# Splitting GpSimd's addition for the softmax sum into three pieces, in the attention of an audio tower on one Trainium2 core

## The chip, the cores and the metric

One Trainium2 chip, one NeuronCore of it. TensorE (PE) multiplies matrices into PSUM, VectorE (DVE), ScalarE (ACT) and GpSimd (POOL) work elementwise, SyncE (SP) starts transfers. The engines run their own instruction streams and meet at semaphores. The metric is the device time of one execution of the whole program, in microseconds (us); lower is better.

## The reference

The program is a small audio tower over 16 clips of 746 frames with 128 features: a convolution over 5 frames with batch norm, a delta-rule attention, an expert-choice FFN, a cross attention against 64 videos of 12 frames each, and a routed FFN. The change is in the cross attention, which comes down to this:

```python
t = layer_norm(text_embeds, ln1_g, ln1_b)        # the tower's rows, T = 16 clips, Nw = 746 rows each
vd = layer_norm(video_embeds, ln1_g, ln1_b)      # V = 64 videos, Fr = 12 frames
q = (t @ Wq.T + bq).reshape(T, Nw, HEADS, HEAD_DIM)      # 2 heads of 64
k = (vd @ Wk.T + bk).reshape(V, Fr, HEADS, HEAD_DIM)
v = (vd @ Wv.T + bv).reshape(V, Fr, HEADS, HEAD_DIM)
logits = jnp.einsum('avhd,bthd->abhvt', k, q) / math.sqrt(HEAD_DIM)
weights = jax.nn.softmax(logits, axis=3)         # over the 12 frames of a video
attn = jnp.einsum('avhd,abhvt->abhtd', v, weights)
attn = attn.mean(axis=0)                         # over the videos
o = attn @ Wo.T + bo
```

So for each of the tower's rows, head and video there is a softmax over 12 frames. Its sum is what the change is about.

## The kernel before, in words

The rows of the 16 clips are cut into 96 chunks (NCH), six a clip: five of 128 rows and one of 106. The attention phase goes over the chunks n = 0 to 95 in one software pipeline that each engine has unrolled for itself. The 128 partitions hold 2 heads x 64 videos; the free dimension holds the 12 frames (FR) times the chunk's rows.

The stations of chunk n, with their lines:

- TensorE writes the logits for 12 frames into three PSUM banks (L1710, 24 matmuls, interleaved with the 24 of the weighted values of chunk n-4, L1718). Two sets of three banks alternate.
- VectorE takes the negated maximum over the frames (L1607) into `nm`.
- TensorE adds `nm` to the logits in PSUM, three matmuls for four frames each (L1737, semaphore `shifted`).
- ScalarE takes the exponential in three instructions for four frames each (L1658) into `eb[:, n % 4]` in SBUF; each raises `e_ready` by one.
- GpSimd adds frames 0 to 5 and frames 6 to 11 in one addition (L1681) into `t1[:, n % 2]`, six partial sums a row. It waits for all three exponentials of the chunk, and, as `t1` has two buffers, for VectorE to have read the partial sums of chunk n-2 (`summed`). It raises `tree`.
- VectorE adds up the six partial sums (L1603) into `den`, once `tree` allows.
- ScalarE turns `den` into its reciprocal by a logarithm and an exponential (L1667, L1669).
- VectorE multiplies the 12 frames of exponentials by it in place (L1612), semaphore `w_ready`.
- TensorE multiplies by the values (L1718), ScalarE copies the result (L1648), TensorE multiplies by Wo and adds the bias (L1748, L1749), ScalarE copies that out (L1644).

VectorE's order is fixed: in its step n it does the sum of chunk n-2, the maximum of chunk n, the multiply of chunk n-2. TensorE's step n is the block of logits n and values n-4 (it first waits for the multiply of chunk n-4), then in some steps a transposition (L367) or a query projection (L1688) for the next clips, then the shift of chunk n-1, then the output of chunk n-5. ScalarE's step n does the copies, the exponentials of chunk n-1, the logarithm and its inverse for chunk n-2, and in some steps three normalizations (L1623) for the next clips. GpSimd has nothing but the addition.

Of the kernel before, what the change touches and what calls it, by code (L numbers as in the profile page):

```python
# [7 lines left out]
ALU = mybir.AluOpType  # L8
# [1516 lines left out]
def attention_phase(nc, k):  # L1525
# [6 lines left out]
    with stack:  # L1532
# [4 lines left out]
        t1 = sb("t1", [P, 2, P, 6])  # L1537
# [7 lines left out]
        q_ps, q_ready, q_bias, l_ps, m_ready, shifted, e_ready = (  # L1545
            sem(x) for x in ("q_ps", "q_ready", "q_bias", "l_ps", "nm_ready", "shifted", "e_ready"))
        tree, summed, rd_ready, w_ready, a_ps, a_ready, o_ps, o_ready = (
            sem(x) for x in ("tree", "summed", "rd_ready", "aw_ready", "a_ps", "a_ready", "ao_ps", "ao_ready"))
        logged = sem("logged")
        ST = 2 * NC  # L1550
        FB = FR // 3
# [5 lines left out]
        def lbanks(n):  # L1557
            o = 3 * (n % 2) * 512
            return k.psf[:, o:o + FR * P].rearrange("p (v t) -> p v t", t=P)
# [4 lines left out]
        def wide(n):  # L1564
            return rows(n % NC)
# [13 lines left out]
        with nc.Block() as block:  # L1579
            @block.vector  # L1580
            def _(dve):
                nc.vector.tensor_scalar(bq8[:], k.bq[:, 0:1], 0.125, None, ALU.mult).then_inc(q_bias, 1)
                nc.vector.memset(ones[:], 1.0).then_inc(q_bias, 1)
                nc.vector.tensor_copy(bparts[:, 0, :], k.bo1[:, :]).then_inc(q_bias, 1)
                for s in range(2):
                    rest = k.bo1[:, :] if s == 0 else rd[:, 0, :]
                    dve.wait_ge(q_bias, 2 * s + 3)
                    nc.vector.tensor_tensor(rd[:, s, :], rest, bparts[:, s, :], ALU.subtract).then_inc(q_bias, 1)
                    dve.wait_ge(q_bias, 2 * s + 4)
                    nc.vector.tensor_copy(bparts[:, s + 1, :], rd[:, s, :]).then_inc(q_bias, 1)  # L1590
                nc.vector.tensor_scalar(bo3[:, :], bparts[:, 0, :], k.ident[:, 0:1], None, ALU.mult).then_inc(q_bias, 1)
                for s in (1, 2):
                    dve.wait_ge(q_bias, 7 + s)
                    nc.vector.scalar_tensor_tensor(out=bo3[:, :], in0=bparts[:, s, :], scalar=k.ident[:, s:s + 1],
                                                   in1=bo3[:, :], op0=ALU.mult, op1=ALU.add).then_inc(q_bias, 1)
                for n in range(NCH + 2):
                    w = n - 2
                    if 0 <= w < NCH:
                        dve.wait_ge(tree, w + 1)
                        m = wide(w)  # L1600
                        if w >= 2:
                            dve.wait_ge(logged, w - 1)
                        nc.vector.tensor_reduce(den[:, w % 2, 0:m], t1[:, w % 2, 0:m, :], AX_X,  # L1603
                                                ALU.add).then_inc(summed, 1)
                    if n < NCH:
                        dve.wait_ge(l_ps, n + 1)
                        nc.vector.tensor_reduce(nm[:, n % 2, 0:wide(n)],  # L1607
                                                lbanks(n)[:, :, 0:wide(n)].rearrange("p v t -> p t v"), AX_X,
                                                ALU.max, negate=True).then_inc(m_ready, 1)
                    if 0 <= w < NCH:  # L1610
                        dve.wait_ge(rd_ready, w + 1)
                        nc.vector.tensor_tensor(eb[:, w % 4, :, 0:m], eb[:, w % 4, :, 0:m],  # L1612
                                                rd[:, w % 2, None, 0:m].to_broadcast([P, FR, m]),
                                                ALU.mult).then_inc(w_ready, 1)
                dve.wait_ge(o_ready, NCH)
# [58 lines left out]
            @block.gpsimd  # L1674
            def _(pool):
                for n in range(NCH):
                    e, m = eb[:, n % 4], wide(n)
                    pool.wait_ge(e_ready, 3 * n + 3)
                    if n >= 2:
                        pool.wait_ge(summed, n - 1)  # L1680
                    nc.gpsimd.tensor_tensor(t1[:, n % 2, 0:m, :].rearrange("p t v -> p v t"), e[:, 0:6, 0:m],  # L1681
                                            e[:, 6:12, 0:m], ALU.add).then_inc(tree, 1)

            @block.tensor
            def _(pe):
# [721 lines left out]
```

## Time and profile before

| | us |
|---|---|
| median of 3 runs | 2271.65 |
| lowest and highest | 2266.53, 2272.15 |
| the profiled execution | 2271.49 |
| its span in the profile | 2269.7 |
| attention phase in it | about 1070 to 1524 |

The profile records one execution of the program. Engines are named PE, PEld (TensorE's loading of weights), DVE, ACT and POOL; L12 is line 12 of the kernel. A group of instructions is told with its count, the time that it keeps its engine busy, the mean duration of one in ns, and the idle time of the engine just before it with what ended that idle time. In a timeline a row is a run of equal instructions: when it starts (in us from the span's start), how long it lasts, and in brackets how long the engine sat idle before it and which instruction released it. Ends of matmuls are modelled, so a row of PE may end slightly after the next has started.

### The profile page before, as it was taken

Reading aid. Unit: us, or ns where it says so; the run is one execution under the profiler, and the core shown is the slowest. Engines: PE = TensorE matmul, PEld = TensorE weight load, DVE = VectorE, ACT = ScalarE, POOL = GpSimd, SP = SyncE. Lnnn points to the kernel's source line nnn. Section 1 sums busy time; section 2 is a strip of 40 time slices with the busy share of each in tenths; the row PEclk is TensorE's granted clock in tenths of the full one; section 3 lists DMA queues with packets and bytes.
Section 4 is the critical chain, followed back from the end, with each engine's and each line's share of the span. In section 5 each row is a group of like instructions: output and inputs, shape, how many; then the busy total and the mean of one; then the engine's idle time right before and its main releaser. Section 6 shows DMA issues by size and latency. Waiting matters only on the chain. (4 is left out here: it accounts for less than half of the span.)

```text
span 2269.7 us, 54561 instructions
## 1 busy us (share of the span) xinstructions
PE 2015.7 (89%) x20890; PEld 1786.3 (79%) x20890; DVE 1604.5 (71%) x4095; ACT 1071.8 (47%) x2699; POOL 602.3 (27%) x649
## 2 busy tenths in 40 slices
PE   6699999989746888996999999986999999999998
PEld 5488777779545787884777777766999999999998
DVE  4755555663583765665999999986777777777774
ACT  4433333332344565652676777753444444444443
POOL 0002222220005545520333334333212212221220
PEclk9699999999976999997999999997999999999999
DMA  8100000000221111100000000000000000000000
GB/s 186 43 1 12 11 12 11 11 11 1 67 59 40 41 34 40 40 22 1 3 3 3 3 3 3 3 3 1 8 14 7 7 7 14 7 7 14 7 8 15
DMA packets 80354, 44.50 MB, mean 20 GB/s; under 512 B 45800, under 2 KB 74024, under 8 KB 79752
## 3 DMA queue, kind: packets, MB, share of 16 engines
q1 hardware_dynamic: 74248, 29.53, 5.7%
q0 software_dynamic: 5888, 12.07, 2.0%
q8 instruction: 136, 2.23, 0.4%
q14 instruction: 82, 0.67, 0.1%
HBM read 27.20 MB, written 14.38 MB: 18 GB/s over the span
## 5 line engine op out<-in xcount | busy, mean ns | idle before, releaser
L2127 ACT ACTIVATE w<-banks,b 128x384 f32<-128x384 f32 (+1 forms) x512 | 259.3, 571 | 392.9 <-PE banks L2202 392.9
L2184 PE MATMUL banks<-w,w 128*128 128x128 f32 (+1 forms) x3072 | 364.1, 275 | 0.0
L2184 PEld LDWEIGHTS banks<-w,w 128*128 128x128 f32 (+1 forms) x3072 | 350.4, 189 | 9.1 <-issue 8.7
L1710 PE MATMUL banks<-qT,w 64*64 64x128 f32 (+1 forms) x4608 | 268.0, 269 | 13.2 <-DVE eb L1612 8.7
L1710 PEld LDWEIGHTS banks<-qT,w 64*64 64x64 f32 x4608 | 247.4, 134 | 31.0 <-issue 20.8
L1718 PE MATMUL banks<-eb,w 64*64 64x128 f32 (+1 forms) x4608 | 268.9, 270 | 1.0 <-DVE eb L1612 1.0
L1681 POOL TENSOR_TENSOR t<-eb 128x768 f32<-128x768 f32 x96 | 172.0, 1791 | 289.2 <-ACT eb L1658 286.6
L1718 PEld LDWEIGHTS banks<-eb,w 64*64 64x64 f32 x4608 | 244.1, 133 | 1.7 <-DVE eb L1612 1.5
L2024 DVE SCALAR_TENSOR_TENSOR h<-banks,t_wt,h 128x128 f32 (+3 forms) x672 | 183.5, 341 | 83.3 <-PE banks L2184 79.8
L1237 POOL DMA_INDIRECT xg<-xs,rowu x184 | 178.8, 972 | 127.5 <-DMA xg<-xs,rowu 83.6
L1612 DVE TENSOR_TENSOR eb<-eb,rd 128x1536 f32<-128x1536 f32 x96 | 210.8, 2196 | 2.3 <-ACT rd L1669 2.3
L2200 PE MATMUL banks<-t_xh,t_w1h 128*128 128x384 f32 (+1 forms) x512 | 182.4, 356 | 0.5 <-ACT w L2106 0.5
L2202 PE MATMUL banks<-t_xh,t_w1l 128*128 128x384 f32 (+1 forms) x512 | 171.4, 335 | 0.0
L1607 DVE TENSOR_REDUCE nm<-banks 128x128 bf16<-128x1536 f32 x96 | 162.8, 1696 | 11.4 <-PE banks L1710 11.4
L2201 PE MATMUL banks<-t_xlo,t_w1h 128*128 128x384 f32 (+1 forms) x512 | 170.8, 334 | 0.0
L2067 POOL TENSOR_TENSOR t_rstd<-t_nv,t_minus_half 128x6 f32<-128x6 f32 x48 | 63.6, 1325 | 393.9 <-DVE t_nv L1925 392.5
L1658 ACT ACTIVATE eb<-banks 128x512 f32<-128x512 f32 (+1 forms) x288 | 146.9, 586 | 0.6
L1183 DVE SCALAR_TENSOR_TENSOR x_yl<-banks,gates,x_yh 128x128 fp32r<-128x128 f32 x184 | 52.0, 344 | 132.7 <-ACT x_yh L1330 128.0
L1428 PE MATMUL banks<-x_sel,x_yh 128*128 128x374 f32 (+1 forms) x384 | 119.3, 392 | 2.1 <-ACT x_oT L1339 2.1
L1191 DVE TENSOR_SCALAR x_sel<-iota,place 128x748 fp32r<-128x748 f32 x184 | 106.6, 633 | 4.0 <-PE banks L1428 4.0
L729 ACT ACTIVATE DT<-banks 128x768 f32<-128x768 f32 x60 | 48.6, 810 | 123.4 <-PE banks L822 123.4
L1428 PE MATMUL banks<-x_sel,x_yl 128*128 128x374 f32 (+1 forms) x384 | 98.9, 339 | 0.0
(305 smaller groups left out, 4261.3 us busy)
## 6 DMA issues: line engine op xcount, KB each, us to landing
out<-h SPq DMA_DIRECT2D x16, 320.0 KB
xs<-r_xl SPq DMA_DIRECT2D x16, 192.0 KB, 2.7
h<-in_xT SPq DMA_DIRECT2D x4, 750.0 KB, 14.9
h<-in_xT SPq DMA_DIRECT2D x4, 749.0 KB, 17.9
xg<-xs,rowu POOLq DMA_INDIRECT x184
xs<-r_xl SPq DMA_DIRECT2D x16, 128.0 KB
blocks<-NT SPq DMA_DIRECT2D x24, 48.0 KB, 1.9
D<-blocks SPq DMA_DIRECT2D x24, 48.0 KB, 2.0
```

The costliest lines, as they stand in the source:

```text
L1237: nc.gpsimd.indirect_dma_start(out=xg[:, 4 * g + j, :], out_offset=None, in_=k.xs, in_offset=bass.IndirectOffsetOnAxis(ap=rowu[:, col:col ...
L1428: last = nc.tensor.matmul(k.ps[:, 5 + s, 0:TW // 2], y[lo:hi, col % 8, :], sel[lo:hi, col % SEL, s * (TW // 2):(s + 1) * (TW // 2)], start ...
L1612: nc.vector.tensor_tensor(eb[:, w % 4, :, 0:m], eb[:, w % 4, :, 0:m], rd[:, w % 2, None, 0:m].to_broadcast([P, FR, m]), ALU.mult).then_inc ...
L1681: nc.gpsimd.tensor_tensor(t1[:, n % 2, 0:m, :].rearrange("p t v -> p v t"), e[:, 0:6, 0:m], e[:, 6:12, 0:m], ALU.add).then_inc(tree, 1)
L1710: last = nc.tensor.matmul(lbanks(n)[place(n, hd), v, 0:wide(n)], k.Kt[half(hd), v, :], qT[half(hd), n // NC % 2, (n % NC) * P:(n % NC) * P ...
L1718: last = nc.tensor.matmul(k.ps[half(hd), 6, 0:wide(a)], k.Vd[place(a, hd), v, half(hd)], eb[place(a, hd), a % 4, v, 0:wide(a)], start=(v = ...
L2024: last = nc.vector.scalar_tensor_tensor(out=hh, in0=k.psf[0:n, o:o + P], scalar=wt[0:n, par, c * E1 + e:c * E1 + e + 1], in1=hh if e else ...
L2127: nc.scalar.activation(gb[u % 2][:, f, s * GW:s * GW + NFREE[s]], k.ps[:, order.bank(n), 0:NFREE[s]], ACT.Relu, bias=k.b1_1[:, 2 * e + f:2 ...
L2184: last = nc.tensor.matmul(k.psf[0:n, o:o + P], gb[u % 2][:, f, c * P:c * P + n], k.w2_1[:, 2 * e + f, :], start=(f == 0), stop=(f == 1))
L2200: nc.tensor.matmul(ps, w1h[:, 2 * e + f, :], xh[:, g, 0:w], start=True, stop=False)
L2201: nc.tensor.matmul(ps, w1h[:, 2 * e + f, :], xlo[:, g, 0:w], start=False, stop=False)
L2202: nc.tensor.matmul(ps, w1l[:, 2 * e + f, :], xh[:, g, 0:w], start=False, stop=True).then_inc(full, 1)
```

## The change

GpSimd's addition of chunk n becomes three. Each waits for one of ScalarE's exponentials (four frames), adds the first two of its frames to the last two, and writes two of the six partial sums. The pairing of the frames becomes another one, the sum of all twelve is the same. VectorE now waits for three counts of `tree` a chunk. The wait for `summed` comes ahead of the first piece.

```diff
                     if 0 <= w < NCH:
-                        dve.wait_ge(tree, w + 1)
+                        dve.wait_ge(tree, 3 * w + 3)
                         m = wide(w)
...
                 for n in range(NCH):
                     e, m = eb[:, n % 4], wide(n)
-                    pool.wait_ge(e_ready, 3 * n + 3)
                     if n >= 2:
                         pool.wait_ge(summed, n - 1)
-                    nc.gpsimd.tensor_tensor(t1[:, n % 2, 0:m, :].rearrange("p t v -> p v t"), e[:, 0:6, 0:m],
-                                            e[:, 6:12, 0:m], ALU.add).then_inc(tree, 1)
+                    for s in range(3):
+                        pool.wait_ge(e_ready, 3 * n + s + 1)
+                        v = s * FB
+                        nc.gpsimd.tensor_tensor(t1[:, n % 2, 0:m, 2 * s:2 * s + 2].rearrange("p t v -> p v t"),
+                                                e[:, v:v + 2, 0:m], e[:, v + 2:v + 4, 0:m], ALU.add).then_inc(tree, 1)
```

`FB` is 4, the frames of one exponential.

## Rows read from the trace of the kernel before

**Rows 1.** The page, sections 1 and 5: engines, and the multiply.

```profile
PE 2015.7 (89%) x20890; PEld 1786.3 (79%) x20890; DVE 1604.5 (71%) x4095; ACT 1071.8 (47%) x2699; POOL 602.3 (27%) x649
...
L1612 DVE TENSOR_TENSOR eb<-eb,rd 128x1536 f32<-128x1536 f32 x96 | 210.8, 2196 | 2.3 <-ACT rd L1669 2.3
```

**Rows 2.** Busy time by window: stretch, length, each engine, TensorE's clock, DMA.

```profile
1200.00:1300.00 100.00, 95.31 (x2266) 74.65 (x2257) 100.00 (x66) 69.46 (x188) 39.30 (x22) 1.00 0.01 3
```

**Rows 3.** Waits of TensorE, 1100 to 1490 us: total, times, longest.

```profile
PE banks L1710 <- DVE eb L1612: 7.2, 14, 0.5
```

**Rows 4.** Waits, 1490 to 1524 us, the drain.

```profile
PE banks L1710 <- DVE eb L1612: 1.0, 3, 0.5
PE banks L1718 <- DVE eb L1612: 1.0, 3, 0.4
```

**Rows 5.** Timeline of VectorE, 1280 to 1300 us.

```profile
1284.50 2.20 DVE L1612 TENSOR_TENSOR eb<-eb,rd 128x1536 f32<-128x1536 f32 x1
1286.63 0.94 DVE L1603 TENSOR_REDUCE den<-t 128x128 f32<-128x768 f32 x1
1287.49 1.74 DVE L1607 TENSOR_REDUCE nm<-banks 128x128 bf16<-128x1536 f32 x1
1289.16 2.49 DVE L1612 TENSOR_TENSOR eb<-eb,rd 128x1536 f32<-128x1536 f32 x1
...
1293.83 1.78 DVE L1612 TENSOR_TENSOR eb<-eb,rd 128x1536 f32<-128x1536 f32 x1
...
1298.06 1.74 DVE L1612 TENSOR_TENSOR eb<-eb,rd 128x1536 f32<-128x1536 f32 x1
```

**Rows 6.** Timeline of GpSimd, 1280 to 1300 us.

```profile
1283.26 1.83 POOL L1681 TENSOR_TENSOR t<-eb 128x768 f32<-128x768 f32 x1 [2.82 <-ACT eb L1658]
1288.21 1.84 POOL L1681 TENSOR_TENSOR t<-eb 128x768 f32<-128x768 f32 x1 [3.11 <-ACT eb L1658]
1292.16 1.84 POOL L1681 TENSOR_TENSOR t<-eb 128x768 f32<-128x768 f32 x1 [2.12 <-ACT eb L1658]
```

**Rows 7.** Timeline of TensorE, 1282 to 1311 us, around the starts of blocks.

```profile
1282.36 0.33 PE L1710 MATMUL banks<-qT,w 64*64 64x128 f32 x2
...
1290.80 0.44 PE L1749 MATMUL banks<-wo,aT 128*128 128x128 f32 x2
1291.75 0.33 PE L1710 MATMUL banks<-qT,w 64*64 64x128 f32 x2 [0.51 <-DVE eb L1612]
...
1295.14 0.44 PE L1749 MATMUL banks<-wo,aT 128*128 128x128 f32 x2
1295.66 0.33 PE L1710 MATMUL banks<-qT,w 64*64 64x128 f32 x2
...
1310.01 0.33 PE L1710 MATMUL banks<-qT,w 64*64 64x128 f32 x2
```

**Rows 8.** Exponentials: timeline of ScalarE, then their group, 1085 to 1520 us.

```profile
1286.57 1.56 ACT L1658 ACTIVATE eb<-banks 128x512 f32<-128x512 f32 x3
...
1290.51 1.57 ACT L1658 ACTIVATE eb<-banks 128x512 f32<-128x512 f32 x3
...
L1658 ACT ACTIVATE eb<-banks 128x512 f32<-128x512 f32 x235 | 122.7, 598 | 0.6
```

**Rows 9.** GpSimd's additions by shape: count, busy us, mean ns, idle us before.

```profile
L1681 POOL TENSOR_TENSOR t<-eb 128x768 f32<-128x768 f32 x80 | 147.0, 1837 | 251.7 <-ACT eb L1658 249.1 <-DVE den L1603 2.6
...
L2078 POOL TENSOR_TENSOR t_ol<-t_ol,g 128x384 f32<-128x384 f32 x32 | 33.0, 1030 | 21.4 <-DVE t_ol L1935 21.4
L2080 POOL TENSOR_TENSOR t_ol<-t_ol,b3n 128x384 f32<-128x384 f32 x32 | 32.0, 1001 | 2.5
...
L1681 POOL TENSOR_TENSOR t<-eb 128x636 f32<-128x636 f32 x16 | 25.0, 1560 | 37.5 <-ACT eb L1658 37.5
...
L645 POOL TENSOR_TENSOR Db<-eye,Nb 96x256 f32<-96x256 f32 x6 | 5.2, 858 | 278.7 <-DMA Nb<-blocks 278.7
...
L653 POOL TENSOR_TENSOR Db<-Db,outer 96x56 f32<-96x56 f32 x12 | 3.5, 293 | 0.9
```

## The prediction

> **What bounds the kernel now.** I read the page first. TensorE leads with 2015.7 us of 2269.7, and VectorE's multiply in attention (L1612) has a mean of 2196 ns [rows 1]. The change touches attention alone, so I asked for a window of it: between 1200 and 1300 us TensorE is busy 95.31 and VectorE 100.00 of 100 us at full clock, GpSimd 39.30 [rows 2]. Two engines look like the bound; the waits say which end last. Over fourteen groups of six chunks TensorE waits 7.2 us for VectorE's multiply, 14 times, at most 0.5 [rows 3]; in the drain it waits 1.0 + 1.0 more [rows 4]. So what any change of the softmax sum can give back is about this wait, however full VectorE looks: behind it TensorE's own work is the floor.
>
> Then the rows of one group, chunk by chunk. The reader is to see a pattern that repeats to 0.01 us. A block (logits of chunk n interleaved with values of chunk n-4) starts at 1282.36 for n = 46, and the same place in the next group (n = 52) starts at 1310.01: 27.65 us for six chunks [rows 7]. In it TensorE stops twice. Before the block at 1291.75 (n = 48) its last matmul ended at 1290.80 + 0.44 = 1291.24: 0.51 idle. Before the block at 1295.66 (n = 49) it was free at 1295.14 + 0.44 = 1295.58: 0.08 idle, too short for the table of waits. The group's floor is 27.65 - 0.59 = 27.06 us.
>
> What ended both stops is a multiply: 1289.16 + 2.49 = 1291.65 and 1293.83 + 1.78 = 1295.61 [rows 5]. Why are they this long? The multiply at 1298.06 took 1.74; GpSimd's additions of rows 6 end before it starts. Those at 1284.50, 1289.16 and 1293.83 were issued while an addition ran, and each ends 1.61 after that addition: 1283.26 + 1.83 = 1285.09 and 1286.70; 1288.21 + 1.84 = 1290.05 and 1291.65; 1292.16 + 1.84 = 1294.00 and 1295.61 [rows 5, 6]. The multiply (two operands in SBUF) does nothing until the addition (two operands in SBUF) is over. The max on PSUM stays at 1.74 under the same additions. So TensorE's wait is pinned to the end of an addition, and the addition to ScalarE: it starts 0.08 after the third exponential (1286.57 + 1.56 = 1288.13, then 1288.21) [rows 6, 8].
>
> **The change, part by part.** *Removed:* the wait for all three exponentials. The first ends one mean, 0.60, after its start [rows 8]: at 1287.17 instead of 1288.13, so GpSimd may start 0.96 us earlier. It is idle then, so nothing is in its way.
>
> *Added:* two more instructions, 256 elements a partition each instead of 768. No row has this shape in this use. 768 elements took 1837 ns and 636 took 1560 (128 and 106 time steps), 2.10 ns an element and 226 fixed; 384 took 1030 in L2078 and 1001 in L2080, 56 took 293 in L653, so 2.25 or 2.16 an element [rows 9]. By the first pair a third costs 226 + 256 x 2.10 = 0.76 us, by L2078 and L653 293 + 200 x 2.25 = 0.74, by L2080 and L653 0.72, the lower bound. The upper bound is the 96x256 row itself, 0.86. A gap between two instructions of GpSimd: L2080, which waits for L2078, sat idle 2.5 us over 32, 0.08 each; where the semaphore has long been raised it may be nothing. I take 0.74 and 0.04 a gap, so 3 x 0.74 + 2 x 0.04 = 2.30 for the sum against 1.84. Starting 0.96 earlier and lasting 0.46 longer, it ends 0.5 earlier. Bounds: 3 x 0.72 = 2.16 (ends 0.64 earlier) and 3 x 0.86 + 0.16 = 2.74 (ends 0.06 earlier). The exponentials come 0.5 apart, faster than the pieces, so only the first piece ever waits for ScalarE.
>
> *Moved:* the wait for the earlier sum now stands ahead of piece one. VectorE had read the sums of two chunks before (1286.63 + 0.94 = 1287.57) 3.6 us ahead of the first piece at 1291.19 that reuses their buffer, so it costs nothing; the cover is that distance [rows 5]. No DMA, no order of another queue moves.
>
> *What it is worth, in the group of the rows.* Pieces start at 1287.17 + 0.08 = 1287.25 and end at 1289.55; the multiply ends at 1291.16, and block 48 can start 0.10 later (1291.65 to 1291.75 is that step): 1291.26 against 1291.24. The wait of 0.51 falls to 0.02. Next, the exponentials at 1290.51 are not moved, since they precede block 48. First one ends 1291.11, pieces 1291.19 to 1293.49, multiply 1295.10, block 49 at 1295.15. TensorE's own time from block 48 to the end of its work is 1295.58 - 1291.75 = 3.83, so it would be ready at 1295.09: 0.06 is left. The group saves 0.59 - 0.08 = 0.51. Both waits occur 15 times (blocks 6 to 90): 15 x 0.51 = 7.7 us.
>
> The multiply must also be issued in time. VectorE's steps are 0.86 (sum, 1286.63 to 1287.49), 1.67 (max, to 1289.16) and 1.67 (multiply without a block) [rows 5]: 4.20 a chunk, 25.2 a group, below 27.06. It has almost 2 us of room a group, which the blocking eats; what is late next is TensorE itself.
>
> *Drain.* The last chunks carry no normalization, TensorE needs some 3.9 a chunk and VectorE 4.2, so VectorE binds and an earlier sum only removes the overlap. Of the 2.0 us waited there [rows 4] I take 0.5 (bounds 0 and 1.0).
>
> Sum: 7.7 + 0.5 = 8.2 us off 2271.49 (the profiled execution, span 2269.7), hence **2263.3**; the median 2271.65 is within 0.2 of it.
>
> A rule against the change: by the Trainium skill, "SBUF — State Buffer", section "Who interferes with whom", a VectorE instruction with two SBUF inputs and a GpSimd one that reads SBUF exclude each other, and whoever issues first holds the shared ports for its whole instruction. The trace agrees for an addition that came first (1.61 above); no row has a multiply first. By this rule a multiply could slip ahead of a piece and hold the rest back 1.74, a case priced below from rows.
>
> **Rivals.** *The pieces are dear:* each costs the 96x256 row's 0.86 plus 0.08. The sum ends at 1287.25 + 2.74 = 1289.99, block 48 starts at 1291.70, and a group saves 0.06 or so: 15 x 0.06 = 1 us, 2270.5. For: GpSimd's small instructions have the largest fixed share. Against: 56 elements took only 293 ns, so that fixed share is at most 0.2 [rows 9]. This is also the case in which the change gains nothing of what it is made for.
>
> *Full recovery:* pieces at 0.72 without gaps, or multiplies that go between pieces and need not wait for the third. All 0.59 and the drain's 1.0: 15 x 0.59 + 1.0 = 9.9 us, 2261.6.
>
> *Slower, the multiply goes first:* today each addition holds the ports through; three leave gaps. No row has a multiply first, so I take the blocking as mutual: a piece issued under a multiply waits for its end. Suppose the multiply of block 48 is issued just before piece one, at 1287.2, ends at 1288.95, and the pieces, at the dear price, run from there to 1291.7. The next sum starts 1291.8, max (short chunk, 1.4) ends at 1294.05, but the following chunk's pieces started only at 1291.7 and end 1294.45; that multiply ends 1296.06, block 49 at 1296.1 against 1295.66 today: 0.45 lost a group, 15 x 0.45 = 6.8 us, 2278.3. At 0.74 a piece the same order gives 1288.95 + 2.30 = 1291.25, sum and max until 1293.6, pieces until 1293.55, multiply until 1295.35: still 0.3 gained. So it decides only from about 0.85 a piece, and only if VectorE runs over 1 us ahead. A late sum would also hold ScalarE's logarithm and the copies behind it, which feed TensorE.
>
> **How the numbers follow.** Forecast (2262 to 2265) 0.52; full recovery 0.12; dear pieces or half the gain 0.28; multiply first 0.08. A measurement of this kernel can't tell less than 0.3%, 6.8 us. Faster than that: the full case and most of the forecast, 0.57, since the group's gain needs only 0.42 of 0.59. Same: dear pieces, half gains and the forecast's lower edge, 0.35. Slower 0.08. The range 2260 to 2271 leaves out the multiply-first case and the far end of each side.
>
> **What would show it.** 288 additions at L1681's place, 0.7 to 0.8 us each, GpSimd's time there from 147.0 + 25.0 = 172 to some 215 us [rows 9]. TensorE's wait for the multiply in the steady stretch from 7.2 to under 2 us, and the group from 27.65 to about 27.14. Multiplies still ending 1.61 after the last piece that blocked them. It is wrong if a piece takes over 0.85; if a multiply starts inside the gaps and the following piece shows 2.4 us instead of 0.74; if the sums over t1 start waiting for GpSimd often; or if TensorE finds another wait in the place of the one removed, on ScalarE's copies first.

## The result and the profile after

The changed kernel takes 2258.51 us (median of 6 runs, 2256.72 to 2259.81) against 2270.85 for the kernel before (6 runs, 2266.53 to 2272.15): a ratio of 0.995, 95% interval 0.994 to 0.996, so 9 to 14 us faster. The forecast was 2263.3, with a range from 2260 to 2271. The direction and the mechanism held; the time lies 1.5 us below the range.

First, how much of it lies where the change is. The attention phase, from the first block of logits to the start of the last block of values, in the timelines of TensorE. Before:

```profile
1069.88 3.46 PE L1710 MATMUL banks<-qT,w 64*64 64x128 f32 x30 [0.76 <-ACT qT L1629]
...
1521.32 0.91 PE L1718 MATMUL banks<-eb,w 64*64 64x106 f32 x15
```

And after, where the same instructions are two lines further down:

```profile
1066.99 6.24 PE L1712 MATMUL banks<-qT,w 64*64 64x128 f32 x72 [0.76 <-ACT qT L1629]
...
1508.07 0.67 PE L1720 MATMUL banks<-eb,w 64*64 64x106 f32 x10
```

1521.32 - 1069.88 = 451.4 us before, 441.1 after: 10.4 us less. What lies behind is the same to 0.1 us (2269.7 - 1521.3 = 748.4 and 2256.4 - 1508.1 = 748.3). Ahead of attention this profile is 2.9 us shorter; the repeat (e0) shows whether that is of the change.

Busy time by window after, for the stretch of [rows 2]:

```profile
1200.00:1300.00 100.00, 97.63 (x2339) 77.08 (x2330) 98.20 (x68) 71.52 (x194) 46.59 (x68) 1.00 0.01 3
```

TensorE rose from 95.31 to 97.63 of 100 us. VectorE, which had no idle time before, now has 1.80 us of it: between 1100 and 1480 us its multiply waits 5.1 us in all for ScalarE's reciprocal, of which more at the end. TensorE's waits after, 1097 to 1477 us, which answers to [rows 3]; this is the whole list:

```profile
PE banks L1750 <- ACT a_xT L381: 5.8, 28, 0.2
```

The 7.2 us behind the multiply are gone. The 5.8 us for ScalarE's copy (L381) stood in the list before too, as L1748, with the same 28 times: some 0.4 us of a group's floor is this wait and not TensorE's own work. GpSimd and VectorE after, then TensorE at the same two blocks, 48 and 49, as in [rows 5 to 7]:

```profile
1279.93 2.13 POOL L1683 TENSOR_TENSOR t<-eb 128x256 f32<-128x256 f32 x3 [2.81 <-ACT eb L1658]
1283.88 2.12 POOL L1683 TENSOR_TENSOR t<-eb 128x256 f32<-128x256 f32 x3 [1.82 <-ACT eb L1658]
```

```profile
1281.33 2.33 DVE L1612 TENSOR_TENSOR eb<-eb,rd 128x1536 f32<-128x1536 f32 x1
...
1285.83 1.77 DVE L1612 TENSOR_TENSOR eb<-eb,rd 128x1536 f32<-128x1536 f32 x1
```

```profile
1283.43 0.44 PE L1751 MATMUL banks<-wo,aT 128*128 128x128 f32 x2
1283.88 0.33 PE L1712 MATMUL banks<-qT,w 64*64 64x128 f32 x2
...
1287.27 0.44 PE L1751 MATMUL banks<-wo,aT 128*128 128x128 f32 x2
1287.72 0.33 PE L1712 MATMUL banks<-qT,w 64*64 64x128 f32 x2
```

A row "x3" is now the three pieces of a chunk. They end at 1279.93 + 2.13 = 1282.06, and the multiply 1.60 later, at 1283.66; the next at 1286.00 and 1287.60. So the multiply is still held until the last piece is over, as before. But 1283.66 is now ahead of 1283.87, when TensorE is done with its own work, and 1287.60 ahead of 1287.71. Both blocks start at once. The group from block 46 to block 52 runs from 1274.98 to 1302.01, here with the block's first row at each end:

```profile
1274.98 0.33 PE L1712 MATMUL banks<-qT,w 64*64 64x128 f32 x2
...
1302.01 0.33 PE L1712 MATMUL banks<-qT,w 64*64 64x128 f32 x2
```

27.03 us against 27.65: the group lost 0.62. The two waits came 15 times, so fifteen such groups are 9.3 us; the drain (from block 91 to the last one) went from 32.06 to 31.13 us, the first steps (to the start of block 5) from 23.82 to 23.72.

### The profile page after: what moved, and what is told of

The parts are those of the page before. It is cut to its first block and busy times, and to the rows that moved or that the text cites. A ratio compares the mean times of both kernels' runs of the same rounds, so it can differ in the third digit from the quotient of the medians.

```text
span 2256.4 us, 54753 instructions
## 1 busy us (share of the span) xinstructions
PE 2009.5 (89%) x20890; PEld 1782.2 (79%) x20890; DVE 1585.7 (70%) x4095; ACT 1071.1 (47%) x2699; POOL 631.8 (28%) x841
## 5 line engine op out<-in xcount | busy, mean ns | idle before, releaser
L1683 POOL TENSOR_TENSOR t<-eb 128x256 f32<-128x256 f32 (+1 forms) x288 | 199.7, 726 | 250.9 <-ACT eb L1658 213.0
L1612 DVE TENSOR_TENSOR eb<-eb,rd 128x1536 f32<-128x1536 f32 x96 | 192.0, 2000 | 9.3 <-ACT rd L1669 8.1
```

Source lines behind the costliest of these rows:

```text
L1683: nc.gpsimd.tensor_tensor(t1[:, n % 2, 0:m, 2 * s:2 * s + 2].rearrange("p t v -> p v t"), e[:, v:v + 2, 0:m], e[:, v + 2:v + 4, 0:m], ALU. ...
```

## The experiments

Eight kernels. "Attention" is the stretch defined above, "group" the six chunks from block 46, both from each one's own trace.

| kernel | median us | ratio to before, 95% | attention us | group us | attention starts at |
|---|---|---|---|---|---|
| before | 2270.85 | | 451.4 | 27.65 | 1069.9 |
| changed | 2258.51 | 0.995 (0.994 to 0.996) | 441.1 | 27.03 | 1067.0 |
| e0, changed again | 2260.64 | 0.9949 (0.9933 to 0.9966) | 441.0 | 27.03 | 1071.2 |
| e1, three late | 2274.68 | 1.0023 (1.0011 to 1.0036) | 455.3 | 28.04 | 1072.3 |
| e2, two pieces | 2263.80 | 0.9977 (0.9965 to 0.9989) | 446.6 | 27.38 | 1067.4 |
| e3, four pieces | 2275.39 | 1.0026 (1.0015 to 1.0036) | 457.7 | 28.04 | 1068.2 |
| e4, one small | 2259.90 | 0.9945 (0.9928 to 0.9963) | 438.1 | 27.01 | 1071.9 |
| e5, fill | 2255.15 (one run) | | 440.1 | 27.01 | 1064.5 |
| e6, multiply first | 2382.53 | 1.0498 (1.0477 to 1.052) | 569.4 | 35.10 | 1062.1 |
| e7, query in the block | 2270.95 | 0.9998 (0.9987 to 1.0009) | 452.4 | 27.79 | 1072.5 |

The ratios are to runs of the kernel before on the same chip, in two batches: median 2268.87 (29 runs) for e0 to e3 and 2270.37 (17 runs) for e4 to e7; they are not exact quotients of the medians.

### e0: the changed kernel again

> The changed kernel once more, unaltered. In its first profile attention (from the first block of logits to the last block of values) took 441.1 us against 451.4 before, and what lies ahead of attention was 2.9 us shorter as well. Theory: only the 10.4 us in attention belong to the change, and the stages ahead of it vary by some us between executions whatever the kernel. Expected: attention 441.1 within 0.3, the part ahead of it anywhere between 1066 and 1071 us. Rival: the shorter part ahead is of the change too; then it starts attention at 1067.0 within 0.5 again.

Attention took 441.0 us again, and this time started at 1071.2. So the 10.4 us are the change's. The further 2.9 us of the first profile are not: the same kernel started attention at 1067.0 and at 1071.2, and the kernel before at 1069.9, between the two. Over all kernels the last column runs from 1062.1 to 1072.5, though none of them changes anything ahead of attention.

### e1: three pieces, but late

```diff
-                        pool.wait_ge(e_ready, 3 * n + s + 1)
+                        pool.wait_ge(e_ready, 3 * n + 3)
```

> Three pieces, but all of them behind the third exponential. Theory (the end of the last addition alone sets TensorE's wait, through the blocked multiply): the three take 2.12 us where the one took 1.84, so the sum ends 0.28 later than before the change; a group of six chunks takes 27.65 + 0.27 = 27.9 us, attention 456, the whole some 4.5 us more than before: 2275. Rival (smaller additions help by themselves, because the multiply gets in between them or is blocked for less long): no slower than before, 2271 or less.

2274.68, slower than before, as the theory has it: the same three pieces without the early start gain nothing. But the way there was another one. GpSimd (two chunks, then the third piece of the first by itself) and VectorE of e1:

```profile
1291.03 3.64 POOL L1683 TENSOR_TENSOR t<-eb 128x256 f32<-128x256 f32 x3 [2.83 <-ACT eb L1658]
1295.01 2.12 POOL L1683 TENSOR_TENSOR t<-eb 128x256 f32<-128x256 f32 x3 [0.34 <-ACT eb L1658]
```

```profile
1292.41 2.26 POOL L1683 TENSOR_TENSOR t<-eb 128x256 f32<-128x256 f32 x1
```

```profile
1292.27 1.81 DVE L1612 TENSOR_TENSOR eb<-eb,rd 128x1536 f32<-128x1536 f32 x1
1294.71 0.95 DVE L1603 TENSOR_REDUCE den<-t 128x128 f32<-128x768 f32 x1 [0.63 <-POOL t L1683]
1295.58 1.47 DVE L1607 TENSOR_REDUCE nm<-banks 128x106 bf16<-128x1272 f32 x1
1296.97 1.77 DVE L1612 TENSOR_TENSOR eb<-eb,rd 128x1536 f32<-128x1536 f32 x1
```

The three pieces last 3.64 here instead of 2.12. The multiply was issued at 1292.27, during the second piece and before the third was issued (1292.41), and went in between: it waited only for the second piece, ended at 1294.08, and the third piece, now the one that waits, took 2.26 and ended at 1294.67. VectorE then sat idle for 0.63 ahead of its next sum. This is the rival "the multiply goes first" at work: block 48 starts earlier than expected (its wait 0.16, not 0.79), block 49 waits 0.64. The group is 28.04, where 27.9 was expected. The attention time of 455.3 hides some of this, since the first steps (to block 5) took 21.62 us here against 23.82 before, at a higher clock (see e4); with equal first steps it would be 457.5, 6.1 more than before.

### e2: two pieces

```diff
-                        dve.wait_ge(tree, w + 1)
+                        dve.wait_ge(tree, 2 * w + 2)
...
-                    pool.wait_ge(e_ready, 3 * n + 3)
...
+                    for v, k2, ready in ((0, 4, 2), (8, 2, 3)):
+                        pool.wait_ge(e_ready, 3 * n + ready)
+                        nc.gpsimd.tensor_tensor(t1[:, n % 2, 0:m, v // 2:v // 2 + k2].rearrange("p t v -> p v t"),
+                                                e[:, v:v + k2, 0:m], e[:, v + k2:v + 2 * k2, 0:m],
+                                                ALU.add).then_inc(tree, 1)
```

> Two pieces: frames 0 to 7 behind the second exponential (512 elements a partition), frames 8 to 11 behind the third. Theory: the first starts 1.22 us after the start of the exponentials and takes about 1.3, the second ends at 1.22 + 1.25 + 0.74 = 3.2; before the change the sum ended at 3.48, with three pieces at 2.86. So 0.27 earlier, in the range where each us of it is a us a group: 27.65 - 0.27 = 27.4, 15 groups give 4 us and the drain 0.5: 2266. Rival (any earlier start sets VectorE free, and TensorE is the limit at once): as with three pieces, 2259.

The group is 27.38 as expected, and attention 446.6 keeps about half the gain. But the number agrees by luck, for the way to it was not the expected one. Piece two by itself, and then VectorE:

```profile
1284.39 2.27 POOL L1682 TENSOR_TENSOR t<-eb 128x256 f32<-128x256 f32 x1
```

```profile
1284.26 1.80 DVE L1612 TENSOR_TENSOR eb<-eb,rd 128x1536 f32<-128x1536 f32 x1
1286.69 0.95 DVE L1603 TENSOR_REDUCE den<-t 128x128 f32<-128x768 f32 x1 [0.63 <-POOL t L1682]
1287.57 1.47 DVE L1607 TENSOR_REDUCE nm<-banks 128x106 bf16<-128x1272 f32 x1
1288.96 1.75 DVE L1612 TENSOR_TENSOR eb<-eb,rd 128x1536 f32<-128x1536 f32 x1
```

The multiply for block 48 was issued 0.13 ahead of piece two and waited only for piece one, so block 48 starts at once. Piece two then took 2.27, the sum waited 0.63 for it, and the multiply for block 49 came late because VectorE was late, not because an addition held it (1.75 is close to its 1.74 alone). So one wait is left, at block 49. The trace names a releaser for it:

```profile
1289.96 0.22 PE L1750 MATMUL banks<-a_bo,a_ones 128*128 128x128 bf16 x1
1290.02 0.44 PE L1751 MATMUL banks<-wo,aT 128*128 128x128 f32 x2
1290.77 0.33 PE L1712 MATMUL banks<-qT,w 64*64 64x128 f32 x2 [0.31 <-ACT eb L1658]
```

ScalarE's exponential is named, since the block waits for both. But the block's first matmul needs only the first exponential of chunk 47, which ended at 1290.33, before TensorE was free at 1290.46; the multiply ended at 1288.96 + 1.75 = 1290.71, 0.06 ahead of the block, and TensorE started 0.05 to 0.10 behind the multiply in the cases above. So it is the multiply.

### e3: a fourth piece behind the three

```diff
+        spare = sb("spare", [P, P, 2])
...
-                        dve.wait_ge(tree, 3 * w + 3)
+                        dve.wait_ge(tree, 4 * w + 4)
...
+                    if n:
+                        pool.wait_ge(tree, 4 * n)
+                    nc.gpsimd.tensor_tensor(spare[:, 0:m, :].rearrange("p t v -> p v t"),
+                                            e[:, 8:10, 0:m], e[:, 10:12, 0:m], ALU.add).then_inc(tree, 1)
```

> The three pieces of the change, and behind them a fourth addition of the same size whose result nobody uses, but for which VectorE's sum waits. It takes 0.69 more, so the additions end 2.86 + 0.69 = 3.55 us after the exponentials' start against 3.48 before. Theory (the end decides): the whole gain goes, a group takes 27.7, the time is 2271 to 2273. Rival (it is the earlier start, or the earlier sums of the first frames, that helps): some of the 10 us stays, 2265 or less.

All of the gain goes and more: 457.7 us in attention, 6.3 above before, where about 1 was expected. So an early start and early first sums alone are worth nothing while the last addition ends late. How much a late end alone costs e3 doesn't show, since the order changed here too. The rows of e3:

```profile
1288.48 2.12 POOL L1684 TENSOR_TENSOR t<-eb 128x256 f32<-128x256 f32 x3 [2.13 <-ACT eb L1659]
1290.55 2.24 POOL L1688 TENSOR_TENSOR spare<-eb 128x256 f32<-128x256 f32 x1
1292.75 2.12 POOL L1684 TENSOR_TENSOR t<-eb 128x256 f32<-128x256 f32 x3
```

The fourth piece takes 2.24, since a multiply issued at 1290.41 went ahead of it, and the next chunk's pieces queue up behind it without a gap. The group is 28.04, the same as in e1.

### e4: is TensorE the floor

```diff
+                nc.gpsimd.memset(t1[:], 1.0).then_inc(filled, 1)
+                pool.wait_ge(filled, 1)
...
-                    nc.gpsimd.tensor_tensor(t1[:, n % 2, 0:m, :].rearrange("p t v -> p v t"), e[:, 0:6, 0:m],
-                                            e[:, 6:12, 0:m], ALU.add).then_inc(tree, 1)
+                    nc.gpsimd.tensor_tensor(t1[:, n % 2, 0:m, 0:2].rearrange("p t v -> p v t"), e[:, 0:2, 0:m],
+                                            e[:, 6:8, 0:m], ALU.add).then_inc(tree, 1)
```

> One addition behind the third exponential, as before the change, but of 256 elements a partition instead of 768 (it leaves out two thirds of the partial sums, which are ones set once at the start of the phase). It ends 1.64 + 0.74 = 2.4 us after the exponentials' start, earlier than the three pieces' 2.86, and blocks VectorE's multiply for at most 0.7. Theory (with three pieces TensorE's own work is the floor): the group stays at 27.0, attention 440 to 441, the whole as the changed kernel, 2258 to 2260. Rival (VectorE's load is the limit, and each us of block removed there counts): the group falls below 26.5 and the time below 2253.

With two thirds of GpSimd's addition left out the group is 27.01, against 27.03: the floor of TensorE's steps, and the three pieces reach it. Attention came out 3.0 us shorter than in the changed kernel, though, and 2 to 3 shorter than expected. 0.6 of that is in the drain (30.58 against 31.13 us), 0.3 in the groups, and 2.1 ahead of them, where the two differ in something else: over the first 9.28 us of the phase the mean granted clock was 1.00 in e4 and 0.77 in the changed kernel (windows of e4 and of the changed kernel):

```profile
1071.88:1081.16 9.28, 8.68 (x140) 7.88 (x142) 3.77 (x3) 3.14 (x7) 0.74 (x1) 1.00 0.02 4
```

```profile
1066.99:1076.27 9.28, 8.68 (x102) 7.88 (x103) 3.45 (x2) 2.21 (x6) 0.00 (x0) 0.77 0.01 2
```

In the changed kernel the clock was 0.50 (1.2 GHz) over the first 4 us and 1.00 (2.4 GHz) from 1073 us on; in e4, and in e1 too, it was 1.00 from the start. TensorE had done much the same ahead of the phase in both: between 10 and 5 us ahead of the phase it was busy for 0.40 us in the changed kernel and 0.19 in e4, and in the last 5 us for 3.99 and 3.77. Why it got the higher clock in e4 and e1 stays open.

### e5 and e6: who holds whom back

Both take the kernel before and let GpSimd's one instruction also wait for VectorE's maximum, so that it is issued just after the multiply. e6 does no more; e5 also puts a fill in the place of the addition, so the softmax sum is left out.

```diff
                     pool.wait_ge(e_ready, 3 * n + 3)
+                    pool.wait_ge(m_ready, min(n + 2, NCH))
...
-                    nc.gpsimd.tensor_tensor(t1[:, n % 2, 0:m, :].rearrange("p t v -> p v t"), e[:, 0:6, 0:m],
-                                            e[:, 6:12, 0:m], ALU.add).then_inc(tree, 1)
+                    nc.gpsimd.memset(t1[:, n % 2, 0:m, :], 2.0).then_inc(tree, 1)
```

> The kernel before, with two things changed: GpSimd's instruction also waits until VectorE has taken the maximum that stands ahead of its multiply, so that it is issued just after the multiply starts; and it is a fill of the partial sums with a constant (it leaves out the addition, nothing is read). Theory: only an instruction that reads SBUF is held back by the multiply and holds it back; fills take 0.75 us within the multiply, which takes 1.74 each time. Rival (any GpSimd instruction and the multiply exclude each other): the fills take over 2 us.

> The kernel before, whose one addition also waits until VectorE has taken the maximum that stands ahead of its multiply: the multiply is always issued first. Theory (whoever is issued first holds the other back for its whole length): each multiply takes 1.74, each addition 1.84 + 1.5 = 3.3, and VectorE's next sum waits for it: 1.6 + 1.84 + 0.1 + 0.86 + 1.67 = 6.1 us a chunk against 4.6, some 140 us more, 2410. Rival (the multiply doesn't hold the addition back): additions of 1.84, about 4.7 us a chunk, within 10 us of the kernel before.

The rows of e6, GpSimd and then VectorE:

```profile
1299.97 3.22 POOL L1682 TENSOR_TENSOR t<-eb 128x768 f32<-128x768 f32 x1 [2.78 <-DVE nm L1607]
```

```profile
1299.76 1.75 DVE L1612 TENSOR_TENSOR eb<-eb,rd 128x1536 f32<-128x1536 f32 x1
1303.23 0.95 DVE L1603 TENSOR_REDUCE den<-t 128x128 f32<-128x768 f32 x1 [1.72 <-POOL t L1682]
```

The multiply takes its 1.75, the addition 3.22: it ends at 1303.19, 1.68 behind the multiply. So the blocking is mutual, and VectorE pays for it one instruction later, 1.72 us of idle time ahead of the sum. The whole takes 2382.5, less than my 2410: VectorE's steps are 5.6 to 6.0 us long, 35.10 for a group of six, so 5.85 a chunk and not the 6.1 that I multiplied by 96. In e5 the same place looks like this:

```profile
1309.84 0.74 POOL L1682 MEMSET t<- 128x768 f32 x1 [3.90 <-ACT eb L1658]
```

```profile
1309.67 1.76 DVE L1612 TENSOR_TENSOR eb<-eb,rd 128x1536 f32<-128x1536 f32 x1
```

The fill lies wholly within the multiply and neither is longer for it. So GpSimd's fill, which only writes SBUF, isn't held back, and its addition, which reads two operands from it, is. The two differ in operation as well as in reading, and no run takes these apart.

### e7: TensorE's query projection inside the block

```diff
+                        if v == 7 and slot(n - 1):
+                            if n - 5 >= 1:
+                                pe.wait_ge(o_ready, n - 5)
+                            query(*slot(n - 1), 7)
...
-                    if now or before:
+                    if now:
...
-                        if before:
-                            query(*before, 7)
```

> The changed kernel, and TensorE does the query projection of a step inside the block, behind frame 7, instead of behind the block. In 30 steps the bias matmul waits about 0.28 us beyond TensorE's own work for ScalarE's copy of the queries, which could start some 0.5 earlier. Theory (TensorE's steps are the floor and VectorE's chain follows the exponentials): 30 x 0.26 = 8 us less, 2251. Rival (the chain over additions and multiplies has no room left behind the three pieces): TensorE waits for multiplies instead, 2257 or more.

An attempt at the new floor, and both theories missed: attention takes 452.4, 11 us more than in the changed kernel. The time is above the rival's 2257, but not for the rival's reason: between 1100 and 1480 us TensorE never waits for a multiply. TensorE in a query step of e7 (block 50), and then of the changed kernel:

```profile
1303.82 0.33 PE L1712 MATMUL banks<-qT,w 64*64 64x128 f32 x2
...
1305.73 0.91 PE L1690 MATMUL banks<-a_xT,wq 128*128 128x384 f32 x2
...
1307.61 0.82 PE L1741 MATMUL banks<-nm,identb 128*128 128x512 bf16 x3
1308.66 0.22 PE L1752 MATMUL banks<-a_bo,a_ones 128*128 128x128 bf16 x1 [0.23 <-ACT qT L1629]
```

```profile
1292.41 0.33 PE L1712 MATMUL banks<-qT,w 64*64 64x128 f32 x2
...
1295.94 0.81 PE L1739 MATMUL banks<-nm,identb 128*128 128x512 bf16 x3
1296.87 0.22 PE L1750 MATMUL banks<-a_bo,a_ones 128*128 128x128 bf16 x1
```

Block and query together took 1307.61 - 1303.82 = 3.79 in e7 and 1295.94 - 1292.41 = 3.53 in the changed kernel: the block of 64*64 matmuls, cut in two by a pair of 128*128 ones, costs 0.26 more. And the bias matmul waited longer, 1.05 behind the start of the shift instead of 0.93, because ScalarE's copy of the queries still stood behind the copy that waits for the block's end. The two make 0.38 of the 0.39 us by which the step grew (5.33 against 4.94). By the Trainium skill, "TensorEngine Tiling (Array Packing)", section "Key Properties", a change of the tiling mode drains TensorE; the 0.26 would fit one more pair of such changes, but no run here takes them alone.

## Why the prediction was off: the working, step by step

**The step that failed.** The mechanism was right and the sum too small. The saving of a group was put at 0.51 us and measured 0.62, above all because the three pieces were given 2.30 us and took 2.12 (the gap between them); the drain was put at 0.5 and gave 0.93. With these terms as measured the time would be 2261.2. What took it below 2260 was a term put at nothing: the difference between executions outside attention. What came in attention is in fact the rival "full recovery", which had a chance of 0.12: both waits of the group gone, and nearly all of the drain's 1.0.

**The bound: right.** TensorE's wait for a pinned multiply was what could be given back, and TensorE's steps the floor. e4 and e5 show the floor (27.01), e6 that the blocking goes both ways, e5 that a fill is free of it. e1 shows that the pieces without the early start gain nothing, and e3 that the early start with a late last addition gains nothing. That it is the end of the last piece that moved the multiply is read from the rows of before and after (1.61 and 1.60 behind it); no run moves this end by itself, since in e1, e2 and e3 the order of the instructions changed as well.

**The price of a piece: right.** 742 ns measured for 256 elements, 0.74 taken (all pieces of this shape in the changed kernel between 1085 and 1500 us):

```profile
L1683 POOL TENSOR_TENSOR t<-eb 128x256 f32<-128x256 f32 x234 | 165.9, 742 | 196.8 <-ACT eb L1658 158.8 <-DVE den L1603 38.0
```

The "DVE den" there is the wait for `summed`; the count that the piece needs was long there, and what the trace names is only the latest event before it. It cost nothing, as forecast: a chunk's first piece starts 0.14 us behind the first exponential, in the chunks with this name as in the others.

**The gap between pieces: this term was mis-sized.** I took 0.04 us, between 0 and 0.08, from L2080, which waits for its forerunner's result. The pieces don't wait for one another, and three of 0.74 last 2.12 to 2.13: each starts 0.05 before the one ahead of it has ended. The sum 3 x 0.74 + 2 x 0.04 = 2.30 should have been 2.12. It is even less than my lower bound of 2.16. By the Trainium skill, "GPSIMD Engine Reference", section "Instruction dispatch", a core of GpSimd starts its share of the next instruction while others still write; the overlap of 0.05 agrees, though the trace doesn't show the single cores. Against it stands a start 0.14 behind the first exponential (1279.79 and 1279.93) where I took 0.08. Together the sum ended 0.11 us earlier than in my working. That was what had been left of the two waits (0.02 + 0.06), so the group lost 0.59 instead of 0.51.

**A gain that I left out.** Another 0.03 to 0.06 of a group lies in the turn step of block 49, which went from 4.75 to 4.69 us. It holds three normalizations on ScalarE, which stand behind the logarithm, and that had waited for VectorE's sum; with the sum earlier (before, the logarithm idled 0.22 there) ScalarE's copy ahead of the transposition comes earlier. TensorE's loading ahead of the transposition waited 5.9 us in 28 times for that copy before and 5.1 after, 0.06 a group. In e1, e2 and e3, where the sums are late, the step is 4.75 or 4.76 again. I had named ScalarE's copies only as a place where time could be lost. That they gained is read from these steps; no run takes it alone.

**The drain: mis-sized.** 0.5 taken of bounds 0 and 1.0; it gave 0.93.

The sum with what was measured: 15 x 0.62 + 0.93 + 0.1 = 10.3, against 8.2. That would have been 2261.2 from the profiled execution, still inside the range. The last 2.7 us to the measured median lie outside attention (in the two profiles, 2.9 us ahead of it), where executions of one kernel differ by more than that: the median of before itself moved from 2271.65 over 3 runs to 2268.87 over 29, and the changed kernel's second batch (e0) has 2260.64, inside the range. I had set the range's lower end 1.6 us below my case of full recovery and left no room for this. So the miss of 1.5 us below the range is of this size, while the sum of 8.2 against 10.4 in attention is a real error.

**The rival that did not come, and why.** The multiply never went between pieces of one chunk: the longest of the 288 pieces took 0.79 us. It was close. Ahead of block 48, ScalarE's reciprocal, the third piece and the multiply:

```profile
1280.99 0.31 ACT L1669 ACTIVATE rd<-rd 128x128 f32<-128x128 f32 x1
```

```profile
1281.31 0.74 POOL L1683 TENSOR_TENSOR t<-eb 128x256 f32<-128x256 f32 x1
```

The multiply was issued at 1281.33, 0.02 behind the third piece. By VectorE's own steps (1.66 from the start of the max to the multiply, and the max started at 1279.51) it would have come at 1281.17, ahead of that piece. It was held for the reciprocal, which it needs and which ended at 1281.30. In the working the multiply came 0.92 + 1.67 us behind the start of the exponentials; now VectorE runs 0.6 us earlier against them and only ScalarE keeps it back. This is the wait that is new in the changed kernel's list:

```profile
DVE eb L1612 <- ACT rd L1669: 5.1, 14, 0.4
```

The distance repeats, since both start from the first exponential of the next chunk: the third piece starts 1.53 us behind its end, and the reciprocal, behind the other two exponentials and the logarithm on ScalarE, ends 1.52 behind it. In 29 multiplies of the phase the multiply follows the reciprocal by 0.03 and the third piece by 0.02 or 0.03, and in the repeat (e0) it is 29 again. In e1, e2 and e3 the pieces come later against the exponentials or are longer or more, the multiply goes first, and a piece takes about 2.26. So the mechanism was real, at about the price named (2.4), and what kept it away is the reciprocal's place on ScalarE, by 0.02 us. This is read from the traces; no run moves the reciprocal by itself.

## What to carry to other kernels

When two engines hold each other back, look at what ends the blocking, not at how busy the blocked one is: VectorE was at 100 of 100 us and yet only 0.6 us of 27.65 was to be had, because TensorE's own steps stood right behind. Splitting the blocking instruction paid here only where its last piece ended earlier (late pieces cost 0.4 us a group); before splitting, compute the new end and where the other engine's instruction is issued, since it may enter between the pieces and push the rest back by its own length. The time of issue has to be worked out for the kernel after the change: when a wait goes, every engine behind it runs earlier, and another one may come to decide the order. And a gain of 10 us in a program whose other stages vary by 10 is best read from the stage's own start and end, with the clock of both looked at.

## What the runs showed of the hardware

- VectorE's two-input multiply and GpSimd's two-input addition held each other back in both directions, for whole instructions and in the order of issue: the multiply ends 1.61 us after the addition that it found running (before); an addition of 1.84 issued 0.2 behind a multiply takes 3.22 (e6).
- GpSimd's fill of 768 elements beside the same multiply costs neither anything that matters (0.74, and 1.76 against 1.74 alone).
- A multiply issued while a piece runs waits for that piece alone; a further piece issued 0.13 or 0.14 behind the multiply takes 2.26 or 2.27 (e2, e1), and one issued 0.02 ahead of it goes first (the changed kernel).
- Three additions of 256 elements in a row on GpSimd take 2.12 us, 0.1 less than the sum of their durations (the changed kernel).
- The clock that TensorE was granted over the first 4 us of attention was 1.2 GHz in the changed kernel and 2.4 GHz in e4, where TensorE's instructions up to there are the same; the steps to block 5 took 23.72 and 21.63 us.
- A pair of 128*128 matmuls put inside a run of 64*64 ones cost 0.26 us more than behind it (e7).
